# A three-stage decoder layer on one core: two input transfers are cut differently, and all five engines get a new order

## What is computed

```python
x = x + xattn(layernorm(x), ctx, ctx, mask)      # 32 heads, 8 key groups, 257 context rows of 256
x = x + s4(layernorm(x), ...)                    # causal convolution along the 1024 columns, by FFT of a kernel
x = x + lora_experts(layernorm(x), A, B, Wq, keys)  # 64 experts of rank 8, the best 16 by a router, softmax gate
```

## Time and profile before

| | us |
|---|---|
| median of three runs | 1288.2 (1287.83 to 1289.85) |
| profiled execution, its time | 1290.52 |
| profiled execution, its span | 1288.6 |
| granted clock, mean of the span | 0.992 |

### The profile page before, as it was taken

The page is one execution under the profiler, slowest core; times in us unless marked ns, Lnnn a source line. Parts: engine busy times, 40 slices in busy tenths (PEclk is TensorE's granted clock), DMA queues, the critical chain, the costliest instruction groups (busy, mean ns, idle before and its releaser), DMA issues.

```text
span 1288.6 us, 41515 instructions
## 1 busy us (share of the span) xinstructions
PE 1232.9 (96%) x13676; PEld 1083.1 (84%) x13676; DVE 959.7 (74%) x3424; ACT 1122.9 (87%) x3337; POOL 825.4 (64%) x1259
## 2 busy tenths in 40 slices
PE   3679999999999999999999999999999999999997
PEld 2558888888888888888888888888888888888886
DVE  6977777777777777877777777677777877877753
ACT  5889999998999999999999999989999999999841
POOL 4447676776667677666767766676777666777520
PEclk9979999999999999999999999999999999999999
DMA  7443443443344444434544433453443344444210
GB/s 237 134 127 93 151 155 122 130 133 125 119 148 152 124 130 132 129 123 141 155 122 131 147 124 118 134 154 123 131 151 123 122 128 154 132 125 132 61 60 33
DMA packets 150103, 166.38 MB, mean 129 GB/s; under 512 B 58217, under 2 KB 116082, under 8 KB 149890
## 3 DMA queue, kind: packets, MB, share of 16 engines
q1 hardware_dynamic: 149890, 163.72, 40.9%
HBM read 128.50 MB, written 34.08 MB: 126 GB/s over the span
## 4 chain that ended last, share of the span: by engine, by line
PE 76%; DVE 5%; DMA 4%; POOL 4%; ACT 4%; issue 3%; SPq 2%; DVEq 0%; ACTq 0%; POOLq 0%
PE ps_p L562 22%; PE ps_p L633 15%; PE ps_p L661 12%; PE ps_p L648 12%; PE ps_p L594 8%; PE ps_s L574 7%; ACT pr L840 2%; DMA dn<-den 2%; DMA xq<-in_x 1%; POOL lastp L1093 1%; DVE ms L1387 1%; SPq L381 1%; ACT pts L772 1%; DMA vl<-in_ctx 1%; POOL lastp L1103 1%
## 5 line engine op out<-in xcount | busy, mean ns | idle before, releaser
L840 ACT ACTIVATE pr<-ms,negmax 128x256 f32<-128x256 f32 x1024 | 512.6, 504 | 17.3 <-DVE negmax L1387 17.3
L1387 DVE CUSTOM_DVE_ANT_0 ms<-ps_s,neg_mask,last 128x256 f32<-128x256 f32 x1024 | 447.0, 473 | 7.1 <-PE ps_s L574 6.2
L772 ACT ACTIVATE pts<-ps_p 128x512 f32<-128x512 f32 x512 | 298.3, 590 | 45.8 <-PE ps_p L562 29.1
L562 PE MATMUL ps_p<-ident,pr 128*128 128x128 f32 x2048 | 296.5, 280 | 10.4 <-ACT pr L840 5.1
L562 PEld LDWEIGHTS ps_p<-ident,pr 128*128 128x128 f32 x2048 | 229.1, 142 | 48.0 <-issue 17.4
L840 ACT ACTIVATION_READ_ACCUMULATOR pr<-ms,negmax 128x1 f32 x1024 | 199.6, 195 | 0.0
L1061 POOL TENSOR_TENSOR kt<-kr,kt 128x512 fp32r<-128x512 f32 x128 | 164.9, 1288 | 24.1 <-ACT kt L772 24.1
L648 PE MATMUL ps_p<-wa_hi,ut_hi 128*128 128x288 f32 x512 | 159.6, 312 | 1.4 <-DVE ut_lo L1203 1.4
L648 PE MATMUL ps_p<-wa_lo,ut_hi 128*128 128x288 f32 x512 | 151.8, 296 | 0.0
L648 PE MATMUL ps_p<-wa_hi,ut_lo 128*128 128x288 f32 x512 | 151.7, 296 | 0.0
L1203 DVE TENSOR_TENSOR ut_lo<-ps_p,ut_hi 128x512 fp32r<-128x512 f32 x128 | 87.7, 690 | 74.8 <-ACT ut_hi L772 74.5
(11 more groups left out here) (139 smaller groups left out, 2584.6 us busy)
## 6 DMA issues: line engine op xcount, KB each, us to landing
cx<-in_ctx SPq DMA_DIRECT2D x128, 256.0 KB, 3.9
kr<-in_keys SPq DMA_DIRECT2D x128, 256.0 KB, 3.0
xq<-in_x SPq DMA_DIRECT2D x32, 512.0 KB, 4.3
turn_q<-xq SPq DMA_DIRECT2D x32, 512.0 KB, 2.9
qx<-turn_q SPq DMA_DIRECT2D x128, 128.0 KB, 2.9
xr<-in_x SPq DMA_DIRECT2D x32, 512.0 KB, 3.9
out_x<-tmp SPq DMA_DIRECT2D x32, 512.0 KB, 3.2
dn<-den SPq DMA_DIRECT2D x512, 2.0 KB, 2.3
```

Source lines behind the costliest of these rows:

```text
L562: mm = pe.transpose(into[:, j * P:(j + 1) * P], source, ident[:, :])
L772: return act.activation(out, in_, ACT.Copy, scale=scale)
L840: act.activation(pr[:, b % 2, g, :], ms[:, n % MS, :], ACT.Exp, bias=negmax[:, n % MS:n % MS + 1], scale=-1.0, accum_out=den[:, b, g:g + 1 ...
L1387: dve.tensor_tensor_reduce(ms[:, n % MS, :], ps_s[:, g % GPH, g // GPH * SW:(g // GPH + 1) * SW], neg_mask[:, 0:SW], 1.0, last[:, it % 2, ...
```

## The change

**Transfers.** `load_last` becomes one transfer instead of four. `move_q` still makes four transfers of 128 KB, but one per batch over all 128 partitions, where before it was one per group quarter over 32 partitions. The DRAM side of each now has the dimensions (4 quarters, 32 rows, 256 numbers) where it had (32 rows, 4 batches, 256 numbers). Then every engine's order and the PSUM banks are new. The number and the shapes of the operations on the four computing engines stay.

```diff
-                for quad in range(GPH):
-                    sp.dma_start(qx[SEQ * quad:SEQ * (quad + 1), :, :, :, :].rearrange("p b h r d -> p b (h r d)"),
-                                 turn_q.rearrange("b s (q c) -> s b q c", q=GPH)[:, :, quad, :]).then_inc(q_moved, 16)
+                for b in range(BPT):
+                    sp.dma_start(qx[:, b, :, :, :].rearrange("p h r d -> p (h r d)"),
+                                 turn_q[b, :, :].rearrange("s (q c) -> q s c", q=GPH)).then_inc(q_moved, 16)
...
-                for c in range(BPT):
-                    sp.dma_start(vl[SEQ * c:SEQ * (c + 1), tile % 2, :],
-                                 context[tile * BPT + c:tile * BPT + c + 1, 2 * P, :]
-                                 .broadcast_to([SEQ, CTX_DIM])).then_inc(vl_loaded, 16)
+                sp.dma_start(vl[:, tile % 2, :],
+                             context[tile * BPT:(tile + 1) * BPT, 2 * P, :].unsqueeze(1)
+                             .broadcast_to([BPT, SEQ, CTX_DIM])).then_inc(vl_loaded, 16)
...
-    "pair": (1, 0, 0, 1, 0, 2, 0, 3, 1, 0, 1, 1, 0, 3, 1, 0,),
-    "out": (0, 1,),
+    "pair": (1, 0, 0, 1, 0, 2, 0, 3, 1, 0, 1, 1, 0, 3, 1, 3,),
+    "out": (0, 2,),
```

More of the change, by code:

```diff
@@ L461, in iteration @@
                     load_keys(it + 1, 2)
+                    move_q(it + 1)
                 if on(it + 2):
                     load_x(it + 2)
[L464 to L467, removed]
                 move_den(it, 0)
@@ L470, in iteration @@
                     load_keys(it + 1, 3)
[L471 to L480, removed]
+                load_context(it, 1)
@@ new lines, in iteration @@
+                if on(it + 1):
+                    store_last(it + 1)
+            load_x(0); load_s4(); load_mask(); load_router(); load_last(0); load_wide(); load_weight(0)
+            load_weight(1); store_q(0); load_keys(0, 0); load_weight(2); move_q(0); load_x(1); load_keys(0, 1)
+            load_weight(3); store_last(0); load_keys(0, 2); clear_kernel(); load_keys(0, 3); load_context(0, 2)
+            turn_last(0); load_context(0, 0); load_weight(4); load_context(0, 3); load_last(1); load_keys(1, 0)
@@ new lines, in _ @@
+            store_q(1); load_keys(1, 1); load_weight(5); move_q(1); load_keys(1, 2); load_weight(6); load_x(2)
+            load_keys(1, 3); load_context(0, 1); store_last(1); move_den(0, 0); turn_last(1); load_context(1, 0)
+            move_den(0, 1); load_weight(7); move_den(0, 2); move_den(0, 3); load_residual(0); load_keys(2, 0)
+            store_kernel(); load_strip(); load_keys(2, 1); load_last(2); store_q(2); load_context(1, 1)
+            move_den(1, 0); move_q(2); load_x(3); load_context(1, 3); move_den(1, 1); load_keys(2, 2); load_keys(2, 3)
@@ L709, in iteration @@
                 attend(it, 1)
+                scores(it, 2)
                 pair_chunk(it, 5)
                 pair_chunk(it, 6)
-                pair_chunk(it, 7)
                 if on(it - 2):
@@ L740, in _ @@
[L740 to L748, removed]
+            weight_chunk(1, 1); weight_chunk(2, 0); weight_chunk(2, 1); cauchy_sums(); scores(0, 0)
@@ L749, in _ @@
+            strip_part(2); pair_chunk(1, 8); attend(1, 2); attend(1, 3); u_chunk(0, 1); convolve(0, 0, 0, 4)
+            pair_chunk(1, 9); convolve(0, 1, 0, 2); convolve(0, 1, 2, 8); pair_chunk(1, 10); z_chunk(0, 0, 0)
+            z_chunk(0, 1, 0)
             for it in range(HEAD, TAIL):
@@ L756, in _ @@
[L756 to L760, removed]
@@ L761, in _ @@
-            pair_chunk(31, 13); pair_chunk(31, 14); pair_chunk(31, 15); attend(31, 4); attend(31, 5); attend(31, 6)
-            attend(31, 7); experts(30, 1, 0, 2); experts(30, 1, 2, 4); experts(30, 1, 4, 8); out_chunk(31, 0)
-            out_chunk(31, 1); experts(30, 0, 0, 3); experts(30, 0, 3, 4); experts(30, 0, 4, 8); gated_chunk(30)
-            expand(30, 0, 0, 4); expand(30, 1, 0, 2); u_chunk(31, 0); u_chunk(31, 1); expand(30, 1, 2, 4)
-            convolve(31, 0, 0, 4); convolve(31, 1, 0, 8); z_chunk(31, 0, 1); z_chunk(31, 1, 1); experts(31, 1, 0, 8)
@@ L766, in _ @@
-            experts(31, 0, 0, 8); gated_chunk(31); expand(31, 0, 0, 4); expand(31, 1, 0, 4)
+            experts(29, 1, 0, 1); experts(29, 1, 1, 3); experts(29, 1, 3, 4); experts(29, 1, 4, 6)
+            experts(29, 1, 6, 8); pair_chunk(30, 15); pair_chunk(31, 0); pair_chunk(31, 1); attend(30, 4)
+            attend(30, 5); scores(31, 1); attend(30, 6); attend(30, 7); pair_chunk(31, 2); experts(29, 0, 0, 1)
+            experts(29, 0, 1, 3); experts(29, 0, 3, 5); experts(29, 0, 5, 6); pair_chunk(31, 3); out_chunk(30, 0)
@@ new lines, in _ @@
+            experts(29, 0, 6, 8); out_chunk(30, 1); pair_chunk(31, 4); gated_chunk(29); attend(31, 0); attend(31, 1)
+            scores(31, 2); pair_chunk(31, 5); pair_chunk(31, 6); expand(29, 0, 0, 4); expand(29, 1, 0, 2)
+            expand(29, 1, 2, 3); pair_chunk(31, 7); u_chunk(30, 0); pair_chunk(31, 8); scores(31, 3); u_chunk(30, 1)
+            pair_chunk(31, 9); convolve(30, 0, 0, 4); convolve(30, 1, 0, 1); convolve(30, 1, 1, 8); pair_chunk(31, 10)
+            expand(29, 1, 3, 4); z_chunk(30, 0, 0); z_chunk(30, 1, 0); pair_chunk(31, 11); attend(31, 2)
@@ L1517, in iteration @@
                 maximum(it, 2)
+                maximum(it, 3)
                 if on(it - 2):
+                    z_stats(it - 2, 1, odd)
                     z_stats(it - 2, 2, odd)
-                if on(it + 1):
-                    q_stats(it + 1, 2)
-                maximum(it, 3)
                 maximum(it, 4)
@@ L1625, in _ @@
-            maximum(1, 27); maximum(1, 28); q_turn(2, 1); q_stats(3, 0); maximum(1, 29); maximum(1, 30)
-            z_stats(0, 0, 0); maximum(1, 31); second_residual(0, 1, 0); z_low(0, 0); z_low(0, 1); q_stats(3, 1)
+            s4_step(); s4_step(); router_low(); s4_step(); weight_low(0, 0); s4_step(); weight_low(0, 1); q_turn(0, 0)
+            weight_low(1, 0); q_stats(1, 0); weight_low(1, 1); q_turn(0, 1); q_stats(1, 1); weight_low(2, 0)
+            s4_step(); q_stats(1, 2); s4_step(); weight_low(2, 1); s4_step(); maximum(0, 0); maximum(0, 1)
@@ L1642, in _ @@
-            route_step(30, 6); out_half(31, 1); route_step(30, 7); route_step(30, 8); route_step(30, 9); gated(30, 1)
-            gated(30, 0); gated_low(30); u_stats(31, 0); u_stats(31, 1); u_stats(31, 2); third_residual(30, 0, 0)
+            z_stats(29, 1, 1); maximum(31, 0); z_stats(29, 2, 1); maximum(31, 1); maximum(31, 2); maximum(31, 3)
+            maximum(31, 4); route_step(29, 0); maximum(31, 5); route_step(29, 1); maximum(31, 6); route_step(29, 2)
+            route_step(29, 3); maximum(31, 7); route_step(29, 4); route_step(29, 5); normalisers(30)
@@ new lines, in _ @@
+            u_low(30, 1); maximum(31, 24); maximum(31, 25); maximum(31, 26); second_residual(30, 0, 0)
+            maximum(31, 27); maximum(31, 28); maximum(31, 29); maximum(31, 30); maximum(31, 31)
+            second_residual(30, 1, 0); third_residual(29, 1, 1); z_low(30, 0); z_low(30, 1); z_stats(30, 0, 0)
+            z_stats(30, 1, 0); z_stats(30, 2, 0); route_step(30, 0); route_step(30, 1); normalisers(31)
+            route_step(30, 2); route_step(30, 3); route_step(30, 4); route_step(30, 5); out_half(31, 0)
@@ L1644, in _ @@
+            route_step(30, 6); route_step(30, 7); route_step(30, 8); route_step(30, 9); gated(30, 1); gated(30, 0)
+            out_half(31, 1); gated_low(30); u_stats(31, 0); u_stats(31, 1); u_stats(31, 2); third_residual(30, 0, 0)
             u_low(31, 0); third_residual(30, 1, 0); u_low(31, 1); second_residual(31, 0, 1); z_stats(31, 0, 1)
-            second_residual(31, 1, 1); z_stats(31, 1, 1); z_low(31, 0); z_stats(31, 2, 1); z_low(31, 1)
+            second_residual(31, 1, 1); z_stats(31, 1, 1); z_low(31, 0); z_low(31, 1); z_stats(31, 2, 1)
```

425 lines of the change are left out of this document (219 added, 206 removed).

## The result

The changed kernel takes 1397.35 us in the median (1396.09 to 1398.0, 4 runs) against 1288.01 (1285.33 to 1289.85) for the kernel before in the same session. The ratio is 1.0849, 95% interval 1.0828 to 1.0871. Forecast were 1343 us and at most 1385: the direction and the mechanism were right, but the forecast loss of 55 us was half of the 109 that came.

What follows compares the result with a forecast made beforehand. TensorE was taken to bound the kernel. Late q makes the period 37.06 + 2.3 = 39.4, 55.2 us more over 29 iterations; with head and tail at zero the span is 1343.8, the median 1343, range 1274 to 1385.

Steps and rivals of the forecast that it cites:

- What bounds it: TensorE is busy 1083.7 of 1087.4 us over 29 iterations at full clock; an undisturbed iteration takes 37.26 us.
- TensorE's order: Two fewer changes between kinds of matmul per iteration gain 0.2 us (0.05 to 0.3), making the period 37.06.
- The x load: `q_stats(it+2, 0)` comes later on VectorE, so x lands before it is needed and 6.9 us of stalls go.
- SP's order: `move_q` now stands behind `move_den(it, 1)` and begins at 23.6 us into the iteration instead of 19.3.
- The shape of q's transfers: A DRAM side beginning with 4 uses four DMA engines: 6.0 us of transfer, all of q there at 31.9.
- What late q does: q landing at 31.9 makes `z_chunk` on PE 2.3 us late each iteration: period 39.4, 55.2 us more in all.
- The chain of 6.4: VectorE needs 6.4 us from `q_turn(it+1, 0)` to the end of `second_residual(it-1, 1)`, for which `z_chunk` waits.
- head and tail at zero: Before and after the 29 iterations, gains of 2 or 3 us offset late q: zero, plus or minus 4.
- B: Rival: q's transfers spread over engines as before and the new order pays, 1277 us; chance 0.17.
- D: Rival: transfers are quick but new waits, as from the new PSUM banks, eat the gain: 1290 to 1300; chance 0.06.
- C: Rival: four engines carry q, yet hidden, needing 35 GB/s an engine: 1277 to 1288; chance 0.09.
- q by 29.6: q may land until 29.6 us after `scores(it, 0)` without delaying `z_chunk(it-1, 1)` on PE.

Runs made afterwards that it cites:

- e14: e3 with `load_x` moved behind `move_den(it, 0)` and `turn_last(it)` ahead of `store` and a key load: 1268.23 us, ratio 0.9871 to the kernel before.
- e5: The kernel before with `q_stats(it+2, 0)` moved behind `q_turn(it+1, 1)` on VectorE: 1286.88 us, ratio 1.0013.
- e17: e14 with `move_q` issued late, behind `load_keys(it+1, 2)` as in the changed kernel, in the new form: 1371.4 us.
- e1: The changed kernel with `move_q` written as before, four transfers over 32 partitions: 1298.05 us, ratio 1.0097 to the kernel before.
- e18: e17 with `move_q` in the form of before, still issued late: 1282.7 us.
- e8: e7 with `store_last(it+1)` directly behind `load_x(it+2)` in SP's order: 1322.60 us, ratio 1.0303 to the kernel before.
- e7: e3 with `turn_last(it)` first in SP's iteration: 1294.45 us, ratio 1.0062 to the kernel before.
- e3: The changed kernel with `move_q(it+1)` directly behind `store_q(it+1)`, ahead of `move_den(it, 1)`: 1294.08 us, ratio 1.0065 to the kernel before.

## Why the prediction missed the size

- **What bounds it; TensorE's order.** Right. The undisturbed period was forecast as 37.06 and is 37.01 in e14. Scores directly followed by `attend` cost nothing extra (0.91), so the gain was near the upper end.
- **The x load.** Wrong in its cause: e5 does not find the 6.9 us at `q_stats`. The stretch of e14 is 1073.3 where 1074.7 was forecast, so they are gone there, not by the way that was argued.
- **SP's order.** Right in its place, half a us short: 23.6 forecast for `move_q`, 23.85 in most iterations and 24.14 in the mean. (19.9 + 2.41 is 22.3 and not 22.6, a slip that happened to help.)
- **The shape of q's transfers: the step that failed, by its size.** That four engines carry q was right, and their speed too: 20.2 GB/s was read for one, and e14 shows 20.5. The step that failed is "The last contains waiting behind other loads, so I take 6.0", which set the row from x (8.0) aside. From first issue to last landing (by the record of semaphore updates) it takes 9.5 us in the mean, so the term is 9.5 - 2.3 = 7.2 us, 1.2 more an iteration. In e14, with only the small transfers of `move_den` right behind it, it is 8.4 - 2.3 = 6.1, so 6.0 was right for q alone. In the changed kernel keys go out right ahead of q and x right behind, and q does wait. e17, where x does not follow at once, has 8.8.
- **What late q does.** The chain of 6.4 measured 6.6. But the next `scores` start 1.35 us after `z_chunk` in the mean, not 1.0 (1.04 in e14): in many iterations TensorE does this piece at the lower clock. 0.35 us.
- **The sum.** Per iteration 0.5 (issue) + 1.2 (transfer) + 0.1 + 0.35 (clock) = 2.2, times 29 = 64 us. Against it stands "head and tail at zero": they gained 11.6. 64 - 12 = 52, the 52.4 that were missing in the span. The transfer is the largest of these terms, about 34 us.
- **Rivals.** B (spread transfers: 1277) was too kind: e1, with the form undone, is 1298, as q was still late and `last` was a second wait under the first. D had named banks as the new wait; it was a transfer. C is out: it needed 35 GB/s an engine, and e14 shows 20.5. The condition "q by 29.6" held well. In e18 q is taken at 29.7, and TensorE waits for `second_residual` for only 2.4 us in all; most of its 0.6 us an iteration stands elsewhere, ahead of `attend(it-1, 4)` and `pair_chunk(it, 4)`.

## What to carry to other kernels

Read a transfer's access pattern from its outermost dimension: a copy that covers all 128 partitions can still begin with 4 on the DRAM side, and then its time is set by four engines; a landing time missing from the list of issues and a lower count of small packets are the signs. Where one queue issues everything, a late transfer costs nothing up to a threshold and everything beyond it, and removing the longest wait uncovers the next, so judge an order only when no wait is left. An issue that has to wait holds up every load behind it: e8, with `store_last` moved ahead of loads, lost 28 us against e7, and e14, with `load_x` moved behind other issues, is 26 us faster than e3, though it moved `turn_last` as well.

## What was not expected of the hardware

With TensorE idle for some 3 us in each iteration, its granted clock fell to the lower level in 18 of the 29 iterations (0.56 of full speed for the 3.5 us shown; `scores` 1.65 against 0.98 us). PE's busy time is 42 us above that of e14, which has the same TensorE order. Most of this costs nothing, since it only fills time in which TensorE would have waited for q; about 0.3 us an iteration, between `z_chunk` and the next `scores`, lies on the way. And a 512 KB load issued right behind the four slow transfers landed in 7.6 us instead of 4.3, while keys issued elsewhere kept their 3.0; with q early (e14) x is back at 3.8.
